# Layer 0 of a graph network on one core: gathers per chunk, sums with channels on partitions, one-hots on ScalarE

## The reference

```python
h = relu(layernorm(x))
f_src, f_dst, f_v = h @ W_src.T + b_src, h @ W_dst.T + b_dst, h @ W_v.T + b_v
a  = f_src[src] + f_dst[dst]                  # per edge, 128 channels
e  = where(a >= 0, a, 0.2 * a)
ex = exp(e - segment_max(e, dst)[dst])
sa = ex / segment_sum(ex, dst)[dst]
x  = x + segment_sum(f_v[src] * sa, dst)      # then layer 1: edge MLPs, softmax over all edges, sum by dst
```

## Time and profile before

| | |
|---|---|
| median of 3 runs | 3502.27 us (3500.87 to 3504.86) |
| span of the profiled execution | 3499.8 us |
| 0 to about 154 us | prepare |
| about 154 to 1532 us | layer0_edges |
| about 1532 to 1668 us | node_tables |
| from there to 3499.8 us | layer 1 and the end |

### The profile page before, as it was taken

The page is one execution under the profiler, slowest core; times in us unless marked ns, Lnnn a source line. Parts: engine busy times, 40 slices in busy tenths (PEclk is TensorE's granted clock), DMA queues, the critical chain, the costliest instruction groups (busy, mean ns, idle before and its releaser), DMA issues. The chain is left out here.

```text
span 3499.8 us, 76247 instructions
## 1 busy us (share of the span) xinstructions
PE 2791.7 (80%) x17156; PEld 1977.5 (57%) x17380; DVE 2528.0 (72%) x4445; ACT 2041.3 (58%) x4527; POOL 2085.4 (60%) x2160
## 2 busy tenths in 40 slices
PE   1577777777777777744799999999999999958885
PEld 0355555555555555532466666666666666647774
DVE  5699999999999999996345555555554555567776
ACT  6355555555555555545355555555555555568885
POOL 0177777777777777732777777777777777500001
PEclk9899999999999999978899999999999999989997
DMA  2555444554444444413777777777777777647662
GB/s 71 172 143 145 142 142 141 142 144 144 142 139 141 143 141 143 141 34 106 206 218 222 218 218 221 220 218 221 217 222 220 220 220 218 190 132 202 202 202 82
DMA packets 391734, 595.68 MB, mean 170 GB/s; under 512 B 73317, under 2 KB 237855, under 8 KB 391682
## 3 DMA queue, kind: packets, MB, share of 16 engines
q0 software_dynamic: 98304, 268.57, 27.1%
q1 hardware_dynamic: 242626, 247.55, 25.4%
q10 hardware_dynamic: 50752, 78.99, 6.6%
HBM read 501.15 MB, written 93.68 MB: 170 GB/s over the span
## 5 line engine op out<-in xcount | busy, mean ns | idle before, releaser
L1194 POOL DMA_INDIRECT l_G<-rows_d,l_sidx x1024 | 1002.5, 979 | 363.1 <-issue 276.3
L807 POOL DMA_INDIRECT l_G<-rows_d,l_sidx x1024 | 1014.0, 990 | 330.5 <-issue 305.0
L1322 ACT ACTIVATE l_h<-l_H,l_cols 128x512 f32<-128x512 f32 x512 | 350.7, 685 | 557.3 <-PE l_H L1229 540.5
L875 PE MATMUL l_accp<-l_we,l_ohe 128*128 128x256 f32 x2048 | 486.3, 380 | 0.0
L831 PE MATMUL l_A<-ident,l_G 128*128 128x128 f32 x1024 | 172.8, 293 | 380.6 <-DVE l_oht L978 323.0
L1386 DVE TENSOR_TENSOR big<-l_SC,l_b 128x512 f32<-128x512 f32 x256 | 177.1, 692 | 387.9 <-PE l_SC L1258 387.9
L875 PEld LDWEIGHTS l_accp<-l_we,l_ohe 128*128 128x128 f32 x2048 | 371.1, 191 | 40.1
L831 PEld LDWEIGHTS l_A<-ident,l_G 128*128 128x128 f32 x1024 | 111.2, 144 | 482.0 <-issue 243.5
L1258 PEld LDWEIGHTS l_SC<-big,l_h 128*128 128x128 f32 x2048 | 263.6, 191 | 146.8 <-issue 146.8
L1548 PE MATMUL ag_accp<-ag_msg,ag_pick 128*128 128x128 f32 x2048 | 286.5, 288 | 73.7 <-ACT ag_msg L1532 32.9
L903 ACT ACTIVATE l_qe<-l_A 128x512 f32<-128x512 f32 x256 | 153.3, 599 | 325.8 <-PE l_A L834 209.7
(11 more groups left out here) (182 smaller groups left out, 5755.4 us busy)
## 6 DMA issues: line engine op xcount, KB each, us to landing
msg_d<-l_msg ACTq DMA_DIRECT2D x256, 256.0 KB, 2.2
ag_msg<-msg_d SPq DMA_DIRECT2D x256, 256.0 KB, 2.9
l_G<-rows_d,l_sidx POOLq DMA_INDIRECT x2048, 3.3
l_lo<-mark_d SPq DMA_DIRECT2D x256, 128.0 KB, 3.0
l_lo<-code_d SPq DMA_DIRECT2D x256, 128.0 KB
l_in<-in_ea_dram SPq DMA_DIRECT2D x512, 64.0 KB
l_fd<-dst_d SPq DMA_DIRECT2D x256, 96.0 KB, 3.4
l_pd<-dst_d SPq DMA_DIRECT2D x256, 96.0 KB
```

Source lines behind the costliest of these rows:

```text
L807: nc.gpsimd.indirect_dma_start(out=G[:, s, j, :], out_offset=None, in_=rows_d[0][:, :], in_offset=bass.IndirectOffsetOnAxis(ap=sidx[:, hal ...
L875: last = nc.tensor.matmul(accp[b][:, 0:2 * C], oh_e[:, b, j, :], we_t[:, b, j, :], start=(j == 0), stop=(j == TJ - 1), skip_group_check=True)
L1194: nc.gpsimd.indirect_dma_start(out=G[:, s, j, :], out_offset=None, in_=rows_d[1][:, :], in_offset=bass.IndirectOffsetOnAxis(ap=sidx[:, hal ...
L1322: nc.scalar.activation(out_t[:, s % 2, :], in_p[:, :], ACT.Silu, bias=cols[:, col:col + 1]).then_inc(ready, 1)
```

## The change

Six parts, nearly all in layer 0:

1. POOL gathers once per chunk (208 times four DMAs), not per item. It loads from a new table how many items must be done before a slot is free, and says after each chunk's landing that it is there (`here`). Items find their slot through a third field of `items_row`.
2. ACT gets `fetch(3)`: it loads two registers from `items_row` (the slot's place and the chunk's number), waits for the chunk and copies f_src out of the slot to `fs_t`, which `front` now turns.
3. The one-hot moves from DVE to ACT, in two steps: `whose(4)` makes |code - own| of codes without marks, and `spread(3)` makes relu(1 - 2^-60 * that). SP gets a third DMA per item for these codes.
4. `collect` is turned round: the weights [ex | ex*f_v] are the stationary operand and the one-hot the moving one, 2 x 4 matmuls of 128 columns. The sums have channels on partitions, so `scale` works on one column (128x2) in place of 128x256. The column of the turn and the copy `rest_of` go.
5. DVE loads a register in `scale`, `add` and `weigh`, not in `scale` alone.
6. `prepare` makes the tables (8 transposes on PE, two copies and some 20 short operations on DVE, three small DMAs), and `node_tables` turns the quotient back on PE and adds it to X on DVE, not on POOL.

```diff
@@ layer0_edges, POOL
-                            if after(i, U):
-                                hold(pool, pool_passed, (wv_ready, i - U + 1))
...
+                                if after(c, U):
+                                    done = pool.value_load(passed_row[0:1, bass.ds(c - U, 1)], min_val=1, max_val=NI)
+                                    hold(pool, pool_passed, (wv_ready, done))
...
+                            c, v, lp = item(lap, u, -1, 2 * U)
+                            if exists(c, CHUNKS):
+                                hold(pool, pool_passed, (gat[v % U], 16 * TJ * (2 * lp + v // U + 1)))
+                                pool.sem_inc(here, 1)
@@ SP
+                            sp.dma_start(who_t[:, s, :], code_d[bass.ds(off, IT)].partition_broadcast(P)).then_inc(ld[s], 16)
@@ PE
-                                nc.tensor.matmul(av[:, j, :], G[:, s, j, 0:C], ident[:, :], is_transpose=True,
+                                nc.tensor.matmul(av[:, j, :], fs_t[:, b, j, :], ident[:, :], is_transpose=True,
...
-                            nc.tensor.matmul(accp[b][:, 2 * C:3 * C], w_t[:, g, 0:1].to_broadcast([P, P]), ident[:, :],
-                                             is_transpose=True, start=True, stop=True, skip_group_check=True)
-                            for j in range(TJ):
-                                last = nc.tensor.matmul(accp[b][:, 0:2 * C], oh_e[:, b, j, :], we_t[:, b, j, :],
+                            for k in range(2):
+                                for j in range(TJ):
+                                    last = nc.tensor.matmul(accp[b][:, k, :], we_t[:, b, j, k * C:(k + 1) * C], oh_e[:, b, j, :],
@@ ACT
+                        act.wait_ge(zeroed, 3)
...
-                            nc.scalar.activation(who_t[:, s % 2, :], lo_t[:, s, 0:IT], ACT.Abs).then_inc(who_ready, 1)
+                            nc.scalar.activation(far_t[:, s % 2, :], who_t[:, s, :], ACT.Abs, scale=-1.0,
+                                                 bias=mine_bc[:, bass.ds(i, 1)]).then_inc(far_ready, 1)
+                        def spread(lap, u, d):
...
+                            nc.scalar.activation(oht[:, g, :], far_t[:, s % 2, :], ACT.Relu, scale=-FAR_STEP,
+                                                 bias=1.0).then_inc(oht_ready, 1)
+                        def fetch(lap, u, d):
...
+                            at = act.value_load(items_row[0:1, bass.ds(i * FIELDS + 2, 1)], min_val=0, max_val=(U - 1) * SLOT)
+                            count = act.value_load(items_row[0:1, bass.ds(i * FIELDS, 1)], min_val=1, max_val=CHUNKS)
+                            act.wait_ge(here, count)
...
                             link(lap, u, 1)
+                            fetch(lap, u, 3)
+                            spread(lap, u, 3)
                             whose(lap, u, 4)
@@ DVE
-                            nc.vector.tensor_scalar(oht[:, g, :], who_t[:, s % 2, :], mine_bc[:, bass.ds(i, 1)], None,
-                                                    ALU.is_equal).then_inc(oht_ready, 1)
...
+                            nc.vector.tensor_scalar(mine, mine, w_t[:, g, 0:1], None, ALU.mult).then_inc(acc_scaled, 1)
@@ node_tables, PE (the order of one group)
+                        for q in range(GROUPS + 2):
+                            back(q, 0)
+                            back(q, 1)
+                            if q >= 2:
+                                pe.wait_ge(s_h, GB * (q - 1))
+                                turn(pe, (q - 2) * PAIRS)
...
+                            back(q, 2)
```

More of the change, by code:

```diff
@@ L655, in _ @@
                     def _(pool):
-                        for q in range(GROUPS + 2):
-                            if q < GROUPS:
-                                pool.wait_ge(s_quotient, q + 1)
-                                nc.gpsimd.tensor_tensor(X[:, span(q), :], X[:, span(q), :], w[:, span(q), :],
-                                                        ALU.add).then_inc(s_sum, 1)
-                            for g in pairs(q - 2):
-                                low(pool, g - 2)
+                        for g in range(HALF):
+                            low(pool, g - 2)
                         low(pool, HALF - 2)
@@ L668, in _, with back @@
                         pe.wait_ge(s_in, 16)
-                        for q in range(GROUPS):
-                            pe.wait_ge(s_h, GB * (q + 1))
-                            turn(pe, q * PAIRS)
-                            for g in pairs(q):
-                                if g + 1 in pairs(q):
+                        def back(q, k):
+                            if not 0 <= q < GROUPS:
+                                return
+                            n = q * len(PARTS) + k
+                            if k == 0:
+                                pe.wait_ge(s_quotient, q + 1)
+                            if n >= 2:
+                                pe.wait_ge(s_sum, n - 1)
+                            for c in PARTS[k]:
+                                last = nc.tensor.matmul(quo[n % 2][:, c - PARTS[k][0], :], w[:, q * GB + c, :], ident[:, :],
+                                                        is_transpose=True, start=True, stop=True, skip_group_check=True)
+                            last.then_inc(s_turned, 1)
+                        for q in range(GROUPS + 2):
[4 more added lines that the diff above has]
+                                turn(pe, (q - 2) * PAIRS)
+                            for g in pairs(q - 2):
+                                if g + 1 in pairs(q - 2):
                                     turn(pe, g + 1)
                                 product(pe, g)
+                            back(q, 2)
                     @block.scalar
@@ L795, in _, with gather @@
                     def _(pool):
[L796 to L797 removed]
+                        def gather(lap, u):
+                            c, v, lp = item(lap, u, 0, 2 * U)
                             s, half = v % U, v // U
[L799 to L809 removed]
```

225 lines of the change are left out of this document (146 added, 79 removed).

## The result

The changed kernel takes 3483.73 us (median of 4 runs, 3482.23 to 3484.61) against 3501.57 us before (4 runs on the same chip, 3496.12 to 3504.86): ratio 0.995, 95% interval 0.9936 to 0.9963. It is faster by 18 us, where 122 were forecast; the time lies outside the range of 3335 to 3440. The profiled execution has a span of 3482.8 us, 17.0 less than before. From the first and last rows of each stage in the two timelines the 17.0 divide so: `prepare` +12.2 us (POOL's first gather starts at 167.58, before at 155.38), the start of the loop +4.6 (to VectorE's first `add`), the loop -51.6 (255 items at 5.052 us in place of 5.254, from `add` to `add`), `node_tables` +16.6 (last `add` to layer 1's first gather), the rest +1.2.

The account below looks back on a forecast made before the run. POOL (5.25 us an item) and VectorE (5.08) bound the old loop; the ScalarE-TensorE circle would set 4.70 after. 3499.8 - 143 + 6 + 2 + 13 = 3378 us of span, so 3380 us; range 3335 to 3440.

Parts of the forecast that it names:

- POOL, 4.27 us an item: Layer 0's loop: 208 chunks of gathers at 5.25 us spread over 256 items, with POOL's added register load hidden.
- the circle: Layer 0's loop: ScalarE and TensorE waiting on each other set the pace, 4.67 us an item; chance 0.50.
- the rival's reason: Layer 0's loop: POOL's register load is exposed, so POOL sets the pace at 4.85 us an item, 3418 us; chance 0.13.
- the step from `spread` to `front`: Layer 0's loop: semaphore time between ScalarE's one-hot and TensorE's first transpose, 0.06 us.
- x: Layer 0's loop: ScalarE's time from `weights` to `fetch`, register loads included, taken as 1.45 us.
- waits of near-equal engines adding up: Layer 0's loop: waits between three near-equal engines give 4.95 to 5.15 us an item, 3445 to 3495 us; chance 0.08.
- VectorE, 4.57: Layer 0's loop: VectorE's operations, without the one-hot and with the small `scale`, sum to 4.57 us an item.
- its cover for two register loads: Layer 0's loop: VectorE's two new loads, 0.66 us each, hide behind scans and cost nothing; uncovered, VectorE would be at 5.9.
- `prepare`, forecast +6: `prepare`: the source table's pair of copies, 8 transposes and some 20 short operations add 6 us.
- The loop's start, forecast +2: Before layer 0's loop: ScalarE waits for the stage's memsets before its first pass, +2 us, an estimate.
- `node_tables`, forecast +13: `node_tables`: TensorE's turn and products queue behind the division, so VectorE stands 4.3 us in three groups, +13 us.
- the added sums and the contention that went: `node_tables`: VectorE takes over the addition, +8 us; POOL's use of memory beside VectorE ends, -8 us.

Follow-up runs that it names:

- e1: Changed kernel with ScalarE's two register loads for `fetch` made right behind `exps`, ahead of `bring`: 3459.27 us.
- e10: e1 with one operand of `leaky`, the running scan, `gap` and `weigh` in PSUM, leaving only the backward scan two in SBUF: 3427.75 us.
- e11: Changed kernel with its loads where they were and three of four gathers a chunk, a quarter of the messages left out: 3453.53 us.
- e5: e1 with three of four gathers a chunk, a quarter of the messages left out: 3370.30 us.
- e8: e1 with VectorE's register load for `weigh` made twice: costs 45 us.
- e4: Changed kernel with TensorE turning the quotient behind the products of the pairs in `node_tables`, not ahead of them: 3467.82 us.
- e13: e10 with e4's order in `node_tables`, and the backward scan cut in two with `weigh` between the halves: median item 5.11 us.
- e15: e10 with e4's order in `node_tables`, the backward scan whole and `gap` moved ahead of `weigh`: median item 5.11 us.

## Why the prediction was wrong

- **POOL, 4.27 us an item: the step that failed.** It took the gather's 1.31 us from the earlier trace rows as a property of the gather. It was the gather beside VectorE's old order, where 545 of 754 started at moments at which nothing held them. With the new order 498 of 634 start under an operation that holds them, a gather costs 1.56 us, and 3.25 of them at e1's 1.52 us are 4.95, where e1's item is 4.96. That gathers stand behind VectorE is shown by their starts and ends and by e10. Why they fall under its operations more often is only worked out: four that nothing holds take 4 x 1.25 = 5.0 us, more than the circle's 4.93 or VectorE's step of 4.62. POOL's register load, the rival's reason, was hidden as I had it: the idle time before a gather is 0.32 us before and after.
- **The circle, 4.67 us: the mechanism right, two terms mis-sized.** In the medians the step from `spread` to `front` is 0.25 us (taken as 0.06) and x is 1.55 (taken as 1.45, bound 1.6); `front` to `weights` is 1.98 (2.00). The sum is 4.93, and e11 gives 4.926 with POOL out of the way. The 0.06 was read from VectorE to TensorE; no row showed the way from ScalarE. That the loads can't start before `weights` was right: in all 157 items from 400 to 1200 us the first starts 0.26 to 0.35 us behind it.
- **Either error was enough.** The circle alone gives 3453.53 (e11) and the gathers alone 3459.27 (e1), both above 3440.
- **The register load was not mis-sized.** ScalarE's is 278 ns (median; 273 to 288), near VectorE's 305. Rows of line 1006, 400 to 1200 us (ns min/median/max):

```profile
L1006 ACTq FUSED_REGOPS  x314: 60/106/152, 402.3 to 1199.9; - x157
L1006 ACTq TENSOR_LOAD <-items_row x157: 273/278/288, 402.4 to 1199.5; - x157
```

- **One bound or two.** I gave 0.50 to a single circle and 0.08 to waits of near-equal engines adding up, 4.95 to 5.15 us an item and 3445 to 3495 us. That rival's figures came, 5.05 us and 3483.7, but in part by luck: it had engines of 4.27 to 4.67 us whose waits add up, and what came were two bounds of 4.93 and 4.96.
- **VectorE, 4.57:** right (4.60 in e5), and so was its cover for two register loads; e8 shows the price without cover, 0.28 us in VectorE's step (4.90 us in place of 4.62) for a second load in a row.
- **`prepare`, forecast +6, measured +12.2.** VectorE carries nearly all of it: its last operation there ends 12.0 us later. The short operations are a chain in full; the six that make `first_row` alone take from 156.78 to 158.93, 2.15 us:

```profile
156.78 0.38 DVE L675 COPY pr_mine_f<-local 1x256 f32<-1x256 f32 x1
...
158.72 0.28 DVE L681 CAST big<-pr_mine_f 1x256 int32<-1x256 f32 x1
```

- **The loop's start, forecast +2, measured +4.6.** The memsets are followed by a whole pass of the new circle before VectorE can go on: its first `leaky` starts 5.86 us after them, 3.57 in the kernel before. That is half of the 4.6; the other half lies between it and the first `add`.
- **`node_tables`, forecast +13, measured +16.6.** The place was right (e4 gives 16 us back), the queueing on TensorE cost 16.6, not 13; the added sums and the contention that went (L325 now has 417 ns at most 426, where the earlier trace rows had 2.46 us) cancelled as forecast.

## What to carry to other kernels

Before a price is carried over from one kernel to the next, ask what ran beside it: POOL's gathers were read at 1.31 us and paid at 1.56, because more of them started under a VectorE operation that holds them. Where two engines lie within a few per cent of each other at the new bound, forecast the pair: here they were 4.93 and 4.96 us, and relieving one gave 24 or 30 us (e1, e11), both 113 (e5). Cutting the scan in e13 added to VectorE, which came next, and its step went from 4.68 (e10) to 5.11 us: read the start-to-start times of dependent neighbours, not the durations.

## What the runs showed of the hardware that was not expected

- A gather that starts under a VectorE operation with two inputs in SBUF ends a fixed time after that operation, to the hundredth of a microsecond: 0.75 us after a scan, 0.82 to 0.85 after the others. One that starts just ahead is free (178 in the kernel before, 0.95 us at most), so a few hundredths of a microsecond in the order of starts decide over up to 1 us. VectorE did not pay for it in the loop: its scans, where they are whole, last 1.28 and 1.22 us in the changed kernel as in the one before.
- Gathers fall into step with VectorE's item: in the changed kernel 118 of 156 items from 400 to 1200 us have three starts of a gather, in the kernel before 87 of 150 four. In e13 and e15, at 5.11 us, about half have four and the means are 965 and 980 ns; POOL waits for buffers there, so that the longer item alone makes the gathers short is not shown.
- TensorE needed 0.25 us (median; 0.23 to 0.29) from the end of ScalarE's `spread` to its first transpose, more than four times what it took behind VectorE's one-hot (median 0.06).
